# The first two tiles of a feed-forward stage prepared between the heads of the convolution before it

## The chip, the cores and the metric

One NeuronCore of a Trainium2 chip runs the whole program. The metric is device time in microseconds (us) of one execution; lower is better. The engines are TensorE (PE; its weight loads are listed as PEld), VectorE (DVE), ScalarE (ACT), GpSimd (POOL) and SyncE (SP), which here only issues DMAs. Each engine runs its own instructions strictly in order, and they meet through semaphores.

## What is computed

One decoder layer on x of shape (8, 256, 512), in three residual steps. The third and the second matter here.

```python
x = x + attn(layernorm(x), Wq, Wk, Wv, Wo)
x = x + xattn(ctx, ctx, layernorm(x), ssm_kernel, D)      # 32 heads of 8 channels, causal convolutions of length 512
x = x + ffn(layernorm(x), w_gate, w_up, w_down, subln_weight)

def ffn(x):
    gate = bit_linear(x, w_gate); up = bit_linear(x, w_up)   # activations to 8-bit steps by row maximum,
    a = up * square(relu(gate))                              # weights to -1, 0, 1
    a = a * rsqrt(mean(square(a)) + 1e-6) * subln_weight
    return bit_linear(a, w_down)
```

## The kernel before

The program has an attention stage and then one block in which the convolution stage (`convolve`, head by head) and the feed-forward stage (`ffn`, tile by tile) follow each other on every engine.

**Convolution.** There are 32 heads, in pairs: an even head uses buffer 0 of everything and PSUM banks 0 to 3, an odd head buffer 1 and banks 4 to 7. For one head SP loads a Toeplitz matrix (`load_toeplitz`, L754) and the context channels (L759); POOL and ACT form the 36 products of channel pairs (L772, L777 and L920); PE convolves them with 10 matmuls, listed as 20 passes (`convolutions`, L784); ACT empties the upper part of the banks into `ys` (L915, L916) and lays out the queries in `qd` (L927); POOL multiplies a shifted share into `z` (L876); DVE multiplies the rest straight from the banks (`multiply`, L826 and L829) and sums 8 products for each output (`add_up`, L837), into `qo`. `multiply` of head h is the last reader of the banks of head h, so PE may start head h+2 only after it (semaphore `s_z1`, L906). DVE's order is multiply of head h, then add_up of head h-1. ACT also turns the feed-forward's weights into -1, 0, 1, three pieces of 48 in each pair of heads (`ternary`, L935 and L939). ACT's row of a pair is: empty even, squares, piece, queries for the next even head, piece, empty odd, squares, piece, queries for the next odd head. The queries wait for `s_z1` and for POOL's share of the head before (L925, L926). All of it is in hardware loops over pairs (L857, L890, L904, L954, L966); only the last pair stands outside on SP, DVE and ACT.

**Feed-forward.** Its rows are 16 tiles (turns) of 128 rows. The rows of a tile are prepared by a chain: PE transposes the tile's piece of `qo` (L1138); DVE adds it to the residual (`rows_x2`, L1243), takes mean and variance (L1248, L1253, L1257); POOL raises to -1/2 (L1407); DVE normalises (L1263), takes the greatest of each row (L1267) and small factors of it (L1271 to L1280); the row is scaled, rounded to whole numbers and written as bf16 in `xq`; a DMA transpose brings it into `xqt` (`turn_rows`, L1086), which PE needs. The first two tiles need only heads 0 to 15. Before, their chains stand behind the last heads: tile 0 altogether (DVE L1376 to L1395, with the integers on DVE, a transpose on PE, L1144, and a copy on ACT, L1206), tile 1 partly there and partly in turn 0.

A turn has four chunks of 512 columns. For each PE makes gate and up (8 matmuls, L1169), ACT makes relu and its square (L1191, L1193), DVE multiplies the two (`chunk`, L1296), ACT sums squares (L1202), POOL multiplies with the gain (`weigh`, L1411), DVE takes the greatest (`greatest`, L1300). At the end of a tile DVE forms its scale (L1306 to L1326), ACT quantises (L1215), POOL makes bf16 (`integers`, L1419), a DMA transposes it (L1078), and PE multiplies it with the third weight, 16 matmuls at the end of the turn two later (`down`, L1154); DVE adds the result (L1334). In turn t the engines also prepare rows of tiles t+1 and t+2. Turns 0 to 5 and the last two are written out, turns 6 to 13 are a loop (L1049 to L1059).

The buffers of the convolution serve again: `toep` holds the chunks, `kv` the relu results, `big` the weighed tile, the fourth quarter of the weight staging tile `wst` is idle in the convolution, and the gain is loaded over all four quarters in one DMA (L1091) after the last weight piece.

## Time and profile before

| what | value |
|---|---|
| median of 3 runs | 653.18 us (651.61 to 656.78) |
| the profiled execution | 651.45 us, of which the instructions' span is 649.7 us |
| PE busy | 584.2 us, 90% of the span |
| DVE, ACT, POOL busy | 484.3, 457.4 and 363.0 us |
| mean granted PE clock | 0.968 of full speed |

Times in the rows further down are microseconds from the start of the span. A row of a timeline gives start, duration, engine, source line, operation, output and inputs, how many instructions were merged, and in brackets the idle time of the engine before it and what ended that.

### The profile page before, as it was taken

The numbers are of one execution on the slowest core, as the hardware profiler recorded it, in microseconds if no ns is written. First come the engines' busy times: TensorE is split into PE (matmuls) and PEld (weight loads), VectorE is DVE, ScalarE is ACT, GpSimd is POOL, SyncE is SP. The second block draws the span as 40 slices with busy tenths as digits, with TensorE's granted clock in tenths as the row PEclk, the third lists the DMA queues.
The fourth block names the chain that finished last, engine by engine and source line by source line (L and its number), as shares of the span: only waits on it lengthen the run. The fifth ranks groups of instructions, "written<-read, shape, count | busy, mean of one in ns | idle before, by whom it ended". The sixth has DMA issues, their size and how long they took to land.

```text
span 649.7 us, 10218 instructions
## 1 busy us (share of the span) xinstructions
PE 584.2 (90%) x2590; PEld 325.8 (50%) x2590; DVE 484.3 (75%) x936; ACT 457.4 (70%) x783; POOL 363.0 (56%) x327
## 2 busy tenths in 40 slices
PE   5699999999999987979999999965799999999975
PEld 3354453635454542467777777742344434444432
DVE  2737778778878765447877877888889989989860
ACT  1164677676666774178898898864788888888960
POOL 1043626254453625457777777743577777777761
PEclk9889999999999995999999999997899999999997
DMA  8774255546474642055665665532153543533424
GB/s 295 229 226 116 67 118 175 129 161 167 152 212 118 190 106 80 25 159 156 183 181 165 178 185 160 168 88 76 31 106 97 98 99 97 121 97 83 98 66 101
DMA packets 87976, 87.08 MB, mean 134 GB/s; under 512 B 46288, under 2 KB 62160, under 8 KB 87824
## 3 DMA queue, kind: packets, MB, share of 16 engines
q1 hardware_dynamic: 87952, 86.81, 49.2%
q8 instruction: 9, 0.15, 0.1%
q14 instruction: 15, 0.12, 0.1%
HBM read 51.71 MB, written 4.28 MB: 86 GB/s over the span
## 4 chain that ended last, share of the span: by engine, by line
PE 28%; POOL 8%; DVE 8%; issue 6%; DMA 4%; ACT 1%; DVEq 0%; POOLq 0%; SPq 0%; ACTq 0%
PE ps L784 20%; PE ps L1154 5%; POOL big L1411 3%; PE ps L1169 3%; DMA act8t<-ys 3%; POOL ys L1419 2%; DVE toep L1296 2%; DVE st L1248 1%; DVE qo L837 1%; DVE ot L1334 1%; POOL r L1407 1%; DVE x_all L1243 1%; DMA toep<-krows 1%; POOL xq L1426 1%; ACT kv L1193 0%
## 5 line engine op out<-in xcount | busy, mean ns | idle before, releaser
L784 PE MATMUL ps<-kv,toep 128*128 128x288 f32 x640 | 155.8, 406 | 2.0 <-PEq L1482 1.1
L784 PEld LDWEIGHTS ps<-kv,toep 128*128 128x128 f32 x640 | 121.4, 190 | 36.5 <-issue 3.2
L1169 PE MATMUL ps<-wt,xqt 128*128 128x512 bf16 x512 | 120.5, 386 | 13.1 <-DVE toep L1296 6.7
L716 POOL TENSOR_TENSOR pts<-big 128x512 f32<-128x512 f32 x64 | 84.9, 1336 | 58.5 <-ACT big L434 58.2
L434 ACT ACTIVATE big<-ps,kscale 128x512 f32<-128x512 f32 x128 | 85.7, 687 | 43.2 <-PE ps L273 41.2
L1411 POOL TENSOR_TENSOR big<-toep,wst 128x512 f32<-128x512 f32 x64 | 82.7, 1294 | 51.5 <-DVE toep L1296 50.9
L1169 PEld LDWEIGHTS ps<-wt,xqt 128*128 128x128 bf16 x512 | 49.4, 99 | 75.9 <-DVE toep L1296 13.0
L273 PE MATMUL ps<-qx,kx 128*128 128x512 f32 x128 | 76.9, 626 | 9.7 <-DMA qx<-kv 7.9
L837 DVE TENSOR_REDUCE qo<-big 128x2048 f32 (+1 forms) x32 | 72.3, 2259 | 0.0
L593 DVE RECIPROCAL yt<-ps 128x256 f32<-128x256 f32 (+1 forms) x24 | 54.8, 2285 | 20.4 <-PE ps L293 20.4
L1154 PE MATMUL ps<-wt,act8t 128*128 128x512 bf16 x256 | 59.8, 388 | 10.9 <-DMA act8t<-ys 10.0
L772 POOL TENSOR_TENSOR kv<-ctx 128x768 f32<-128x768 f32 (+1 forms) x32 | 52.6, 1644 | 30.0 <-PE ps L784 27.3
L826 DVE TENSOR_TENSOR big<-ps,qd 128x1024 f32<-128x1024 f32 x32 | 39.2, 1224 | 36.5 <-ACT ys L916 34.0
L876 POOL TENSOR_TENSOR big<-ys,qd 128x768 f32<-128x768 f32 x32 | 56.4, 1762 | 14.0 <-ACT ys L916 11.8
L242 PE MATMUL ps<-wq_s,qo 128*128 128x512 f32 x128 | 64.2, 592 | 0.0
L313 PE MATMUL ps<-wo_s,yt 128*128 128x512 f32 x128 | 57.9, 594 | 0.0
L1191 ACT ACTIVATE kv<-ps 128x512 f32<-128x512 f32 x64 | 37.7, 589 | 23.2 <-PE ps L1169 23.1
L273 PEld LDWEIGHTS ps<-qx,kx 128*128 128x128 f32 x128 | 25.0, 199 | 55.7 <-issue 30.9
L1296 DVE TENSOR_TENSOR toep<-ps,kv 128x512 f32<-128x512 f32 x64 | 43.7, 682 | 8.0 <-ACT kv L1193 6.7
L699 POOL TENSOR_TENSOR ro<-ve,half 128x2 f32<-128x2 f32 x8 | 5.5, 692 | 76.8 <-DVE ve L604 76.8
L1154 PEld LDWEIGHTS ps<-wt,act8t 128*128 128x128 bf16 x256 | 24.5, 99 | 44.6 <-DMA act8t<-ys 12.7
L1300 DVE TENSOR_REDUCE mb<-big 128x1 f32<-128x512 f32 x64 | 43.4, 678 | 1.1 <-POOL big L1411 1.0
(127 smaller groups left out, 964.0 us busy)
## 6 DMA issues: line engine op xcount, KB each, us to landing
qx<-kv SPq DMA_DIRECT2D x128, 128.0 KB, 2.4
wst<-in_wall SPq DMA_DIRECT2D x12, 1024.0 KB, 7.1
wst<-in_wall SPq DMA_DIRECT2D x48, 256.0 KB, 3.6
toep<-krows SPq DMA_DIRECT2D x32, 256.0 KB, 3.6
ctx<-in_ctxt SPq DMA_DIRECT2D x32, 192.0 KB, 2.5
qo<-in_xt SPq DMA_DIRECT2D x8, 512.0 KB, 3.9
out_y<-ot SPq DMA_DIRECT2D x16, 256.0 KB, 2.2
conv_part<-qo SPq DMA_DIRECT2D x14, 256.0 KB, 2.8
```

The costliest lines, as they stand in the source:

```text
L242: mm = pe.matmul(MB[:, t, :], rows[:, k, t * P:(t + 1) * P], wq_s[:, k, :], start=(k == 0), stop=(k == CK - 1))
L273: pe.matmul(SB[:, n % 2, :], kx[:, kv, s * P:(s + 1) * P].bitcast(F32R), qx[:, kv, gp * C:(gp + 1) * C].bitcast(F32R), start=True, stop=Tr ...
L313: mm = pe.matmul(OB[:, t, :], yt[:, k, t * P:(t + 1) * P], wo_s[:, k, :], start=(k == 0), stop=(k == CK - 1))
L434: act.activation(pt[:, s, kv, gp * C:(gp + 1) * C], SB[:, n % 2, :], ACT.Exp, scale=kscale[:, c:c + 1]).then_inc(s_e.sem, 1)
L716: nc.gpsimd.tensor_tensor(pts[:, n % 6, :], pt[:, 0, kv, gp * C:(gp + 1) * C], pt[:, 1, kv, gp * C:(gp + 1) * C], ALU.add).then_inc(s_ps.s ...
L784: mm = pe.matmul(m.ps[:, LB * r + lb, :].rearrange("p (b s) -> p b s", s=WIDE)[:, :, 0:PAIRS], m.toep[r][:, d * P:(d + 1) * P], m.kv[r][:, ...
L837: nc.vector.tensor_reduce(qo[:, :, bass.ds(h * HD, HD)], z[r][:], AX.X, ALU.add).then_inc(s_red.sem, 1)
L876: nc.gpsimd.tensor_tensor(z[r][:, :, :, HD - SHIFTS:HD].rearrange("p n j s -> p n s j"), window(ys[r][:], SHIFTS - 1, (SHIFTS * EW, NB), ( ...
L1154: mm = pe.matmul(DB, act8t[r][:, k, :], down_w[:, k, :], start=(k == 0), stop=(k == FK - 1))
L1169: mm = pe.matmul(bank[:, n % 2, :], xqt[r][:, k, :], wt[:, k, n * C:(n + 1) * C], start=(k == 0), stop=(k == CK - 1))
L1296: nc.vector.tensor_tensor(a[n % 2][:], UB[:, n % 2, :], r2[n % 2][:], ALU.mult).then_inc(s_a.sem, 1)
L1411: nc.gpsimd.tensor_tensor(act_w[r][:, n * C:(n + 1) * C], a[n % 2][:], gb[:, n * C:(n + 1) * C], ALU.mult).then_inc(s_w.sem, 1)
```

## The change

The convolution's hardware loops end after head 17 on PE, DVE, POOL and SP (`EARLY = 9` pairs); heads 18 to 31 are written out in the feed-forward's part of each engine. ACT keeps its loop. Into the written-out heads go the two row chains, a step per head:

- PE transposes tile 0's piece of `qo` ahead of head 20 and tile 1's ahead of head 25, each into bank 1 of that head's own four banks; that head then computes its blocks in the order 3, 2, 0 and, after DVE's addition, 1.
- DVE does one step of a chain ahead of the multiply of each head: addition (heads 19 and 24), statistics (20, 25), normalising and greatest (21, 26), factors (22, 27), integers (23, 28). The normalised row goes to SBUF instead of a bank.
- POOL's power stands behind its share of heads 20 and 25.
- SP's DMA transposes of the two rows stand behind the whole SP turn of heads 24 and 25, and between the Toeplitz loads of heads 30 and 31. The PE transpose of tile 0, its copy on ACT and the bf16 identity go.
- PE's turn 0 starts behind head 31 when head 30's banks are free. The transposes for tile 2 follow chunk 1 of turn 0 and wait for the multiply of head 31.
- DVE no longer sums heads 30 and 31 ahead of turn 0: `add_up` of head 30 stands in turn 1 behind chunk 1, that of head 31 in turn 2 behind chunk 3. Two of tile 0's four `greatest` move from turn 0 to turn 1.
- ACT's last weight piece moves into turn 0, between `square` of chunk 0 and the relu of chunk 2; two pieces stand ahead of emptying head 31.
- The gain is loaded in four DMAs, the first early, into the idle quarter, the others behind the last three weight pieces, all ahead of the `conv_part` load for tile 3.
- ACT's and POOL's share of tile 2's integers move to the front of turn 1.

```diff
+EARLY = 9
...
-def convolutions(pe, m, r):
-
-    for lb in range(LB):
+def convolutions(pe, m, r, blocks=range(LB)):
+
+    for lb in blocks:
...
-        with pe.Fori(1, PR) as i:
+        with pe.Fori(1, EARLY) as i:
             for r in range(2):
-                pe.wait_ge(s_z1.sem, 2 * i + r - 1)
-                conv(2 * i + r, r, i + 1)
+                conv(i, r)
+        return ready, conv
...
-        for r in range(2):
-            empty(H2 - 2 + r, r)
-        for s in range(3):
-            ternary(PR - 1, s)
+        empty(H2 - 2, 0)
+        ternary(PR - 1, 0)
+        ternary(PR - 1, 1)
+        empty(H2 - 1, 1)
+        return ternary
...
+    HEAD_TURNED = (20, 25)
+    first_banks = [m.ps[:, 1, :], m.ps[:, LB + 1, :]]
...
+        gain(0)
+        for i in range(EARLY, H2 // 2 - 1):
+            conv_turn(i)
+            if i == 12:
+                turn_rows(0, 0, first=True)
+        toeplitz(H2 // 2 - 1, 0)
+        turn_rows(1, 1, first=True)
+        toeplitz(H2 // 2 - 1, 1)
+        for s in range(3):
+            weights(H2 // 2 - 1, s)
         sp.wait_ge(m.s_red.sem, H2 // 2)
         place(2)
-        sp.wait_ge(m.s_tern.sem, PIECES)
-        sp.dma_start(gb[:], g.rearrange("(o n) -> o n", o=1).broadcast_to([P, FF])).then_inc(d_g.sem, 16)
+        for n in range(1, IC):
+            sp.wait_ge(m.s_tern.sem, PIECES - IC + 1 + n)
+            gain(n)
         place_next(3)
-        turn_rows(1, 1, first=True)
...
-                if n == 0 and rows:
+                if n == (0 if after else 1) and rows:
+                    if not after:
+                        pe.wait_ge(m.s_z1.sem, H2)
                     turn_conv_part(t + 2)
...
-        pe.wait_ge(m.s_red.sem, H2 // 2)
+        for h in range(2 * EARLY, H2):
+            if h not in HEAD_TURNED:
+                conv(h // 2, h % 2)
+                continue
+            t = HEAD_TURNED.index(h)
+            pe.wait_ge(m.s_z1.sem, h - 1)
+            pe.wait_ge(m.s_red.sem, H2 // 2)
+            turn_conv_part(t, qo[:, :, t * T:t * T + P], first_banks[t])
+            ready(h, h % 2, h // 2 + 1)
+            convolutions(pe, m, h % 2, (3, 2, 0))
+            wait(pe, s_x2, t, 1)
+            convolutions(pe, m, h % 2, (1,)).then_inc(m.s_conv.sem, 1)
         pe.wait_ge(m.s_z1.sem, H2 - 1)
-        for t in range(2):
-            turn_conv_part(t, qo[:, :, t * T:t * T + P], first_banks[t])
-        pe.wait_ge(c_ident.sem, 2)
-        turn_first_rows()
...
+            if not after:
+                square(t, 0, after)
+                ternary(H2 // 2 - 1, 2)
             relu(t, 2)
...
+        def first_turn():
+            chunk(0, 0, False)
+            chunk(0, 1, False)
+            rows_x2(2)
+            rows_stats(2)
+            rows_mean(2)
+            rows_var(2)
+            greatest(0, 0, 0)
+            chunk(0, 2)
+            rows_norm(2)
+            chunk(0, 3)
+            rows_greatest(2)
+            rows_scale(2)
...
-            chunk(t, 0, after)
+            chunk(t, 0)
+            if not last:
+                greatest(t - 1, 1, 1 - r)
+                greatest(t - 1, 2, 1 - r)
...
+            chunk(t, 1)
+            if not last:
+                add_up(dve, H2 - 2, 0)
+            scale(t - 1, 1 - r)
...
             chunk(t, 3)
+            if last and not final_first:
+                add_up(dve, H2 - 1, 1)
...
+        for h in range(2 * EARLY, H2 - 1):
+            for t in range(2):
+                first_rows(t, h + 1 - HEAD_TURNED[t])
+            dve.wait_ge(m.s_red.sem, h - 1)
+            multiply(dve, h, h % 2)
+            add_up(dve, h - 1, 1 - h % 2)
+        dve.wait_ge(m.s_red.sem, H2 - 2)
+        multiply(dve, H2 - 1, 1)
         schedule(turn, dve.Fori)
...
+        for h in range(2 * EARLY, H2):
+            if h == HEAD_TURNED[0]:
+                pool.wait_ge(c_half.sem, 1)
+            conv_turn(h // 2, h % 2)
+            if h - 2 in HEAD_TURNED:
+                power(rs, ve, s_ve, s_rs, HEAD_TURNED.index(h - 2))
+        for r in range(2):
+            multiply_shifted(H2 - 2 + r, r)
```

How the order of the instructions moves is shown at three places. Names are `line operation output<-inputs shape`; changed lines have new numbers.

DVE in before, from the multiply of head 31 (L826, L829) to the end of tile 0's rows; x_all is the residual, xq0 the finished row:

```order
L826 TENSOR_TENSOR big<-ps,qd1 128x256x4
L829 TENSOR_TENSOR big<-ps,qd1 128x256
L1253 BN_AGGR mv3<-st 128x2
L1257 TENSOR_SCALAR ve<-mv3 128x1
L837 TENSOR_REDUCE qo<-big 128x32x8
L1263 TENSOR_SCALAR ps<-x_all,mv3,rs 128x512
L1267 TENSOR_REDUCE mx<-ps 128x1
...
L1284 TENSOR_SCALAR xq32<-ps,s127 128x512
L1286 TENSOR_SCALAR xq0<-xq32 128x512
```

DVE now, heads 20 to 23 (L827 and L830 are a multiply, L838 an add_up):

```order
L1271 BN_STATS st<-x_all 128x6
L1276 BN_AGGR mv3<-st 128x2
L1280 TENSOR_SCALAR ve<-mv3 128x1
L827 TENSOR_TENSOR big<-ps,qd0 128x256x4
L830 TENSOR_TENSOR big<-ps,qd0 128x256
L838 TENSOR_REDUCE qo<-big 128x32x8
L1288 TENSOR_SCALAR xq32<-x_all,mv3,rs 128x512
L1292 TENSOR_REDUCE mx<-xq32 128x1
...
L1310 TENSOR_SCALAR xq32<-xq32,s127 128x512
L1312 TENSOR_SCALAR xq0<-xq32 128x512
L827 TENSOR_TENSOR big<-ps,qd1 128x256x4
L830 TENSOR_TENSOR big<-ps,qd1 128x256
```

Each step of the chain now stands ahead of a multiply, that is between an add_up and the instruction that frees PE's banks.

DVE in before, turn 1 from chunk 1 of tile 1 (L1296) to its chunk 2; L1306 begins the scale of tile 0:

```order
L1296 TENSOR_TENSOR toep1<-ps,kv1 128x512
L1306 TENSOR_REDUCE sm<-ss 128x1
L1308 TENSOR_SCALAR cc<-cf_all 128x1
L1311 TENSOR_SCALAR var<-sm,cc 128x1
L1313 TENSOR_REDUCE mb<-mb4 128x1
```

DVE now, the same place (chunk is L1351, the scale begins with L1361):

```order
L1355 TENSOR_REDUCE mb4<-big 128x1 x2
L1266 TENSOR_TENSOR x_all<-ps,x_all 128x512
L1355 TENSOR_REDUCE mb4<-big 128x1
L1271 BN_STATS st<-x_all 128x6
L1351 TENSOR_TENSOR toep1<-ps,kv1 128x512
L838 TENSOR_REDUCE qo<-big 128x32x8
L1361 TENSOR_REDUCE sm<-ss 128x1
```

The sum of head 30 (L838) stands between chunk 1 and the scale, and ahead of chunk 1 stand three `greatest` of tile 0 (L1355) where turn 1 of before has one.

SP in before, from the last pair of heads on (L754 Toeplitz, L852 weight pieces, L1064 the piece of qo for PE, L1091 the gain, L1086 a row transpose):

```order
L754 DMA toep0<-krows 128x512
L754 DMA toep1<-krows 128x512
L852 DMA wst2<-in_wall 128x512 x3
L1064 DMA conv_part<-qo 128x4x128
L1091 DMA wst2<-in_g 128x2048
L1064 DMA conv_part<-qo 128x4x128
L1086 DMA_TRANSPOSE xqt1<-xq1 128x4x128
```

SP now, from the end of the SP turn of heads 24 and 25 to the load for head 27, and from the last pair on:

```order
L853 DMA wst2<-in_wall 128x512
L1098 DMA_TRANSPOSE xqt0<-xq0 128x4x128
L755 DMA toep0<-krows 128x512
L760 DMA ctx0<-in_ctxt 128x384
...
L755 DMA toep0<-krows 128x512
L1098 DMA_TRANSPOSE xqt1<-xq1 128x4x128
L755 DMA toep1<-krows 128x512
L853 DMA wst2<-in_wall 128x512 x3
L1076 DMA conv_part<-qo 128x4x128
L1072 DMA wst2<-in_g 128x512 x3
L1076 DMA conv_part<-qo 128x4x128 x2
```

A row transpose now stands in SP's queue ahead of a Toeplitz load of head 26 and another ahead of that of head 31; three gain loads stand ahead of the `conv_part` load for tile 3.

## Rows read from the trace of the kernel before

**Rows 1.** Stage windows: us, busy time of each engine (instructions), PE clock, DMA share, GB/s
```profile
300.00:431.30 131.30, 131.30 (x543) 102.72 (x543) 105.54 (x84) 113.12 (x186) 97.28 (x79) 1.00 0.57 171
431.30:442.70 11.40, 1.56 (x13) 1.08 (x11) 10.96 (x21) 6.06 (x9) 2.73 (x4) 0.68 0.26 92
468.00:479.40 11.40, 10.94 (x52) 5.04 (x53) 10.51 (x31) 10.51 (x20) 9.00 (x9) 1.00 0.39 81
```

**Rows 2.** Chain of waits, heads 2 to 28 of the convolution on PE
```profile
285.67 131.20 PE ps L784 x540
```

**Rows 3.** Timeline of PE, from the last head to turn 4
```profile
431.24 1.04 PE L1138 MATMUL ps<-ident,qo 128*128 128x128 f32 x8
...
442.74 3.26 PE L1169 MATMUL ps<-wt,xqt 128*128 128x512 bf16 x8 [0.77 <-ACT xqt L1206]
...
455.82 3.55 PE L1169 MATMUL ps<-wt,xqt 128*128 128x512 bf16 x8 [2.64 <-DMA xqt<-xq]
...
467.98 1.90 PE L1169 MATMUL ps<-wt,xqt 128*128 128x512 bf16 x8 [2.99 <-DMA xqt<-xq]
...
475.96 3.63 PE L1154 MATMUL ps<-wt,act8t 128*128 128x512 bf16 x16 [0.46 <-DMA act8t<-ys]
479.42 1.89 PE L1169 MATMUL ps<-wt,xqt 128*128 128x512 bf16 x8
...
490.75 1.89 PE L1169 MATMUL ps<-wt,xqt 128*128 128x512 bf16 x8
```

**Rows 4.** Timeline of DVE, heads 27 and 28
```profile
414.51 1.22 DVE L826 TENSOR_TENSOR big<-ps,qd 128x1024 f32<-128x1024 f32 x1 [1.78 <-ACT ys L916]
415.65 0.62 DVE L829 TENSOR_TENSOR big<-ps,qd 128x256 f32<-128x256 f32 x1
416.11 2.26 DVE L837 TENSOR_REDUCE qo<-big 128x2048 f32 x1
418.55 1.23 DVE L826 TENSOR_TENSOR big<-ps,qd 128x1024 f32<-128x1024 f32 x1 [0.19 <-DVE qo L837]
```

**Rows 5.** Timeline of ACT, heads 27 and 28
```profile
413.30 0.89 ACT L915 COPY ys<-ps 128x768 f32<-128x768 f32 x1
...
420.89 0.62 ACT L927 COPY qd<-qo 128x512 f32 x1 [0.56 <-POOL big L876]
```

**Rows 6.** Timeline of DVE, the row chain behind the last head
```profile
432.88 0.69 DVE L1248 BATCH_NORM_STATS2 st<-x_all 128x6 f32<-128x512 f32 x1
...
437.59 0.80 DVE L1263 TENSOR_SCALAR ps<-x_all,mv,rs 128x512 f32<-128x512 f32 x1
...
439.16 0.15 DVE L1271 TENSOR_SCALAR cl<-mx 128x1 f32<-128x1 f32 x1
...
440.04 0.74 DVE L1284 TENSOR_SCALAR xq<-ps,s 128x512 f32<-128x512 f32 x1
...
441.16 0.68 DVE L1243 TENSOR_TENSOR x_all<-ps,x_all 128x512 f32<-128x512 f32 x1
```

**Rows 7.** DMA issues, 400 to 470 us: KB each, median us to landing
```profile
toep<-krows SPq DMA_DIRECT2D x5, 256.0 KB, 3.8
...
xqt<-xq SPq DMA_TRANSPOSE x2, 2.6
```

**Rows 8.** Timeline of SP, the first row transpose
```profile
453.25 1.30 SPq L1086 DMA_TRANSPOSE xqt<-xq  x1
```

**Rows 9.** Timeline of ACT, weight pieces behind the last head, then turn 0
```profile
432.52 0.82 ACT L935 ACTIVATE wst<-wst,magic,wscale 128x512 f32<-128x512 f32 x1
...
434.07 0.80 ACT L935 ACTIVATE wst<-wst,magic,wscale 128x512 f32<-128x512 f32 x1
...
449.53 0.59 ACT L1191 ACTIVATE kv<-ps 128x512 f32<-128x512 f32 x1
...
450.69 0.61 ACT L1202 ACTIVATE asq<-toep 128x512 f32<-128x512 f32 x1
```

**Rows 10.** Timeline of POOL, the first `integers`, in turn 2
```profile
469.57 1.90 POOL L1419 TENSOR_SCALAR ys<-big 128x2048 bf16<-128x2048 f32 x1
```

More of the change, by code:

```diff
@@ L1042, in schedule @@
     def schedule(turn, fori):
-        turn(0, 0, after=False, last=False)
+        turn(0, 0, after=False, last=False, more=False)
         turn(1, 1, last=False)
@@ L1218, in turn @@
             relu(t, 0)
+            if after and not last:
+                rows_scaled(t + 1)
             if after:
@@ L1221, in turn @@
             relu(t, 1)
-            if more:
+            if more and last:
                 rows_scaled(t + 1)
+            if not after:
+                square(t, 0, after)
+                ternary(H2 // 2 - 1, 2)
             relu(t, 2)
-            square(t, 0, after)
+            if after:
+                square(t, 0)
             square(t, 1)
@@ L1428, in turn @@
         def turn(t, r, after=True, last=True, rows=True, more=True, pair=0, stores=0, final_first=True):
+            if not after:
+                for n in range(IC):
+                    pool.wait_ge(d_g[n].sem, 16)
+                    weigh(t, n, r)
+                    if n == 0:
+                        power(rs, ve, s_ve, s_rs, t + 2)
+                return
+            if not last:
+                rows_integers(t + 1, 1 - r, pair + r)
             weigh(t, 0, r)
             weigh(t, 1, r)
[L1431 to L1434 removed]
+            power(r4, var, s_var, s_r4, t - 1)
+            if more and last:
+                rows_integers(t + 1, 1 - r, pair + r)
             if rows:
```

164 lines of the change are left out of this document (65 added, 99 removed).

## Prediction, made before the changed kernel ran

> **What bounds the kernel now.** I first read the busy time by stages. From 300 to 431 us PE is busy for all of its time at the full clock, 2.4 GHz, so the convolution is bound by PE; the 11.4 us behind it hold 1.56 us of PE work at a mean clock of 0.68, while DVE is busy for 10.96 of them; a later turn of 11.4 us has PE busy for 10.94 and DVE and ACT for 10.51 each [rows 1]. So there are three regimes, and the change moves work from the second into the other two. The chain of waits gives the rhythm of the first: 27 heads in 131.20 us without a gap, 4.86 us each, so head 28 ends at 416.87 and the last at 416.87 + 3 x 4.86 = 431.45, near the 431.24 at which PE goes on with the transposes [rows 2, 3]. I call that end E and count from 431.4. The timeline of PE then shows the turns: turn 0 starts at 442.74, that is E + 11.3; turn 1 at E + 24.4, after a wait of 2.64 us for its row transpose; turn 2 at E + 36.6, after 2.99 us for the same reason; turn 3 at E + 48.0, turn 4 at E + 59.35, so the rhythm is then 11.35 [rows 3]. The first 8 matmuls of turns 0 and 1 take 3.26 and 3.55 us, those of turn 2 take 1.90 [rows 3]: PE had been idle and came back at the lower of its two levels, 1.2 GHz.
>
> **What goes.** The gap from E to turn 0 (11.3 us), the two waits for row transposes (2.64 and 2.99 us) and 1.4 and 1.65 us of slow matmuls. They can't be added up as the gain, since work of DVE and ACT comes back elsewhere. I work out the start of turns 1 to 4 anew instead.
>
> **Turn 0 to turn 1: E + 8.3.** PE starts at E: head 30's multiply is long done, and both row transposes were issued heads before. Of ACT's and DVE's work: emptying head 31 takes 1.2 us (from its start to the multiply that waits for it) [rows 4, 5]; a relu and its square 1.16 [rows 9]. Chunk 0's is thus through at E + 2.5, and chunk 1's at about E + 4, since its gate needs 12 matmuls of 0.24 (8 in 1.90 [rows 3]). Then come square (0.8, with its read-out), the moved weight piece, 434.07 - 432.52 = 1.55, and chunk 2's relu pair: E + 7.5 [rows 9]. DVE's chunk (about 0.7) ends near E + 8.3, and PE's turn 1 waits for that. DVE is not later: head 31's multiply ends at E + 3.1 (1.2 + 1.14 + 0.62 [rows 4]).
>
> **Turn 1 to turn 2: 13.0.** Turn 2 waits for chunk 2 of turn 1, one turn of DVE later. A turn is 10.51 us of DVE [rows 1]; added is the sum of head 30, 2.26 [rows 4]; I add 0.25 for the wait for chunk 3's relu. Turn 2 starts at E + 21.3. The row transpose of tile 2, with 2.6 us to land [rows 7], is ready before: its factors are done at E + 11.5, integers and landing follow in about 4.
>
> **Turn 2 to turn 3: 13.0.** Turn 2 now ends with the first `down`. In before `integers` began 469.57 - 467.98 = 1.6 us after the start of turn 2 and `down` 475.96 - 467.98 = 8.0 after it [rows 3, 10]. DVE's scale of tile 0 is the thing that is late now, behind the sum of head 30: POOL comes to `integers` behind the product of chunk 3, at turn 2 + 3.1, so `down` starts at 9.5, and with its 3.45 us (479.42 - 475.96) turn 3 starts at 13.0 [rows 3], E + 34.3.
>
> **Turn 3 to turn 4: 13.0.** The sum of head 31 is one more 2.26 us of DVE ahead of turn 3's first chunk [rows 4]. DVE was some 0.7 us early then, as PE had waited for `down`, so 11.35 + 2.26 - 0.65 = 13.0. Turn 4 starts at E + 47.3, and from there nothing differs from before. Against E + 59.35 that is 12.0 us won. Each start rests on several such steps, so I hold the 12.0 to within 1.5 either way; the two sums that move out of the gap give 4.5 us back, which is the largest cost.
>
> **Heads 18 to 31: E itself gets later.** (a) PE's 8 transposes, 1.04 us [rows 3], now all stand on the path: +1.04. (b) DVE's pieces. A tile costs 0.68 (addition) + 0.69 and two tiny operations, about 1.0 (statistics) + 439.16 - 437.59 = 1.57 + 440.04 - 439.16 = 0.88 + 441.16 - 440.04 = 1.12, 5.25 in all [rows 6], so 10.5 for both. In a pair DVE is idle for 1.78 ahead of an odd multiply and 0.19 ahead of an even one [rows 4]. So the pieces at odd heads (19, 21, 23, 25, 27) are hidden by the wait for ACT's emptying; those at even heads, 1.0 (20), 0.88 (22), 0.68 (24), 1.57 (26), 1.12 (28), push the multiply. What that costs: an odd multiply ends at 415.65 + 0.62 = 416.27, and PE needs it at 416.87, slack 0.6. An even one has 1.4 for PE, but ACT lays out the next even queries behind it, which now wait 0.56 for POOL [rows 5]; a delay beyond that shifts ACT's next piece and the emptying of the odd head. So about 0.56 + 0.6 less 0.15 for the signal, 1.0, is free. Head 26 exceeds it by 0.5; what is not won back in head 27 adds to head 28's 1.12. I take 1.2 for both. Ends: 0, and 10.5 if every piece stood on the path; 1.2 because only two of ten pieces exceed their slack. (c) SP. A Toeplitz load is issued some 0.4 us after the head before last ends and lands in 3.8 [rows 7], so 0.65 of 4.86 is left. The first row transpose holds SP for 1.30 [rows 8] ahead of head 26's load; 0.5 of that is covered by the transposes ahead of head 25. I take 0.1; the ends are 0 and, were the load to wait for the whole landing of the transpose (2.6 + 3.8 + 0.4 - 5.4 [rows 7]), 1.4. The second transpose goes out before head 31's load is due and costs nothing, by the same count. What (a) to (c) do not show is code written out for 14 heads; turns 0 to 5 are written out too, and their rhythm of 11.35 [rows 3] is that of the loop, so 0. Sum: E + 2.3.
>
> The Trainium skill bears on (c). In "DMA: Bandwidth & Descriptors", Queues, rings and completion order, it says that an engine's descriptors are consumed in ring order, a later one behind an earlier. By that the load of head 26 stands behind the transpose, and the sum would be at the upper end of (c); the rows of before show no load behind a transpose on a path, so they neither confirm nor deny it.
>
> Costs taken as nothing: three gain loads ahead of tile 3's `conv_part` (it is then due at about E + 10, just when turn 1's PE comes to it; if late, DVE still has 3 us before it needs the result); POOL's two powers between heads (POOL is busy for 97.28 of 131.3 [rows 1]); two weight pieces ahead of emptying head 31 (3.1 us into ACT's idle time there; without that cover, as if ACT is late by the delay of (b), some tenths).
>
> **Sum.** -12.0 + 2.3 = -9.7. The profiled execution took 651.45 (span 649.7), so 641.75; from the median, 653.18, 1.7 above it, it is 643.5. I say 643. A measurement here tells about 1%, 6.5 us, from no change.
>
> **Rivals.**
> 1. *The prize is halved by the turns* (gain 3 to 6.5, about 648). PE is busy for only half of turns 1 and 2, with waits of up to 3.4 us, and falls to 1.2 GHz as it did before turns 0 and 1; 1.4 to 1.65 us at up to two restarts [rows 3], and (b) at 2 to 3 instead of 1.2. For it: turn 1 of before came back slow behind its wait. Against: turn 2, behind a like wait, ran at the full clock [rows 3], and DVE, not PE, sets these turns. The Trainium skill ("TensorE: Matmul & The Clock Gate", Part 1) says that an idle array goes to half rate and work brings it back, which agrees with the 0.68 in the gap [rows 1]; by it the sum would lose up to 3.
> 2. *DVE becomes the bound of heads 18 to 31* (slower, about 655). Every delayed multiply delays ACT's queries, ACT's emptying and so the next multiply, and the slack is never won back: all 10.5 us of pieces, 1.04 of transposes and 1.4 of the load make 12.9 against 12.0, and a slow restart adds 1.5. It decides once E is over 12 us later. For it: 105.54 of 131.3 us of DVE and 113.12 of ACT are taken [rows 1]. Against: the gap of 1.78 in each pair.
> 3. *More is won* (gain 13 to 15, about 639): the sums hide where DVE waits for `down`, and the pieces cost nothing.
> 4. *It doesn't do what it says*: turn 0 still waits, for a row transpose that comes late. The second is issued two heads before E; no row speaks for it. Then the gain is 3 or less, 651.
>
> **Chances.** Forecast (gain 6.5 to 13) 0.62; rival 1 0.20; rival 2 0.05; rival 3 0.10; rival 4 0.03. Faster by over 1% are the forecast, rival 3 and a little of rival 1: 0.74. Within 1%: 0.23, slower by over 1%: 0.03. The range goes from rival 3 to the upper part of rival 1: 638 to 649.5.
>
> **What would show it.** Right: heads from 18 on at 4.86 us with about 0.5 more at 20 and 25 and a few tenths at 27 to 31; the first gate matmuls directly behind the last head; turns 1, 2, 3, 4 at about 8, 21, 34 and 47 us after it; add_up in turns 1 and 2. Wrong: PE waits of over 1 us at several heads for DVE's multiply (rival 2), 3 us and more for 8 matmuls in turns 1 to 3 (rival 1), a wait for `toep` at head 26 over 1 us, or a turn 1 later than E + 10.

## The result: 644.2 us, and the profile after

The changed kernel takes 644.2 us (median of 4 runs, 642.72 to 645.77) against 653.38 (4 runs, 651.61 to 656.78) for the one before, measured on the same chip: a ratio of 0.9864, with a 95% interval of 0.9829 to 0.9899. The forecast was 643.0, faster; measured is 1.4% faster. The profiled execution took 645.77 us, its span is 643.9 and its mean granted clock 0.976.

Windows of after, one for the heads from 300 us on and one for each of turns 0, 2 and 4 (columns as in [rows 1]: the stretch, its length, the busy time of PE, PEld, DVE, ACT and POOL with the number of instructions, the granted PE clock, the DMA share, GB/s):

```profile
300.00:439.90 139.90, 138.15 (x567) 105.87 (x567) 118.08 (x114) 119.83 (x196) 102.19 (x84) 1.00 0.59 172
439.90:447.90 8.00, 7.31 (x36) 3.46 (x36) 6.82 (x12) 7.58 (x15) 4.59 (x4) 1.00 0.21 73
...
460.60:473.50 12.90, 12.26 (x51) 5.34 (x53) 12.03 (x33) 12.12 (x21) 10.20 (x10) 0.89 0.35 73
...
486.35:497.70 11.35, 10.93 (x52) 5.00 (x52) 10.48 (x31) 10.09 (x19) 8.63 (x8) 1.00 0.45 104
```

The regime in the middle of [rows 1], 11.4 us with 1.56 of PE at a clock of 0.68, is gone: turn 0 has PE busy for 7.31 of 8.00 us at the full clock. In exchange PE is no longer busy all through the heads (138.15 of 139.90), DVE's busy time there is 118.08, and turn 2 has a clock of 0.89.

The timeline of PE in after, heads 2 to 31 and the start of turn 0, which answers to [rows 2] and the top of [rows 3]:

```profile
289.50 77.84 PE L785 MATMUL ps<-kv,toep 128*128 128x288 f32 x320 [0.81 <-DMA toep<-krows]
367.56 9.94 PE L785 MATMUL ps<-kv,toep 128*128 128x288 f32 x40 [0.21 <-issue]
377.33 0.60 PE L1160 MATMUL ps<-ident,qo 128*128 128x128 f32 x4
377.77 15.00 PE L785 MATMUL ps<-kv,toep 128*128 128x288 f32 x60
392.94 9.97 PE L785 MATMUL ps<-kv,toep 128*128 128x288 f32 x40 [0.18 <-DVE big L830]
402.87 0.66 PE L1160 MATMUL ps<-ident,qo 128*128 128x128 f32 x4
403.36 5.02 PE L785 MATMUL ps<-kv,toep 128*128 128x288 f32 x20
408.57 19.92 PE L785 MATMUL ps<-kv,toep 128*128 128x288 f32 x80 [0.20 <-issue]
429.42 5.12 PE L785 MATMUL ps<-kv,toep 128*128 128x288 f32 x20 [0.93 <-DVE big L830]
434.71 5.12 PE L785 MATMUL ps<-kv,toep 128*128 128x288 f32 x20 [0.17 <-DVE big L830]
439.88 2.32 PE L1182 MATMUL ps<-wt,xqt 128*128 128x512 bf16 x10
```

The row that was unbroken in [rows 2] is cut at heads 18 (367.56), 20 and 25 (the transposes), 23 (392.94), 26 (408.57), 30 and 31. Turn 0 (L1182) follows head 31 with no gap. The timeline of PE over turns 1 to 4:

```profile
447.86 1.89 PE L1182 MATMUL ps<-wt,xqt 128*128 128x512 bf16 x8 [0.69 <-DVE toep L1351]
...
455.35 1.90 PE L1182 MATMUL ps<-wt,xqt 128*128 128x512 bf16 x8 [1.30 <-DVE toep L1351]
460.63 3.25 PE L1182 MATMUL ps<-wt,xqt 128*128 128x512 bf16 x8 [3.38 <-DVE toep L1351]
...
470.06 3.63 PE L1170 MATMUL ps<-wt,act8t 128*128 128x512 bf16 x16 [0.54 <-DMA act8t<-ys]
473.52 1.89 PE L1182 MATMUL ps<-wt,xqt 128*128 128x512 bf16 x8
...
486.35 1.89 PE L1182 MATMUL ps<-wt,xqt 128*128 128x512 bf16 x8
```

The waits ahead of turns 1 and 2, for a row transpose in [rows 3], are now for DVE's chunk; turn 2 comes back at the lower level (3.25 us for 8 matmuls instead of 1.90; a granted clock of 0.55 from 460.60 to 463.72), 1.2 GHz, after a wait of 3.38.

For all kernels below (their times are single runs where no interval stands with them) I use three lengths: the time from the start of head 17 to the start of head 31 (by the single weight loads on PE; "a step" is that from one head to the next), the starts of turns 1 to 4 after E (by the first matmul of each turn; E is the end of head 31's last matmul), and, for the net, from the start of head 2 to turn 4. The expectations recorded ahead of the runs count the turns from weight loads, which gives 8.2 and 21.0 for the 8.0 and 20.8 of turns 1 and 2. The net is 204.90 us before and 196.66 after, 8.2 less. Head 2 began between 284.7 and 289.5 us in the thirteen profiles, and last in after's, though the change does not touch what stands ahead of it; so a single time can't tell 1 or 2 us, and the lengths can. The heads of after stand unchanged in three other kernels here (sums_first, no_sums, warm), and the length of heads 17 to 30 in these four profiles is 72.60 to 72.76: it repeats to 0.2 us. Single steps vary more: that into head 18 takes 5.4 to 5.6 there, and that behind head 20 is the shorter (5.2 to 4.9) the longer it is.

| kernel | time, us | heads 17 to 30 | turns 1, 2, 3, 4 after E |
|---|---|---|---|
| before | 653.4 | 67.91 | 24.4, 36.6, 48.0, 59.35 |
| after | 644.2 | 72.60 | 8.0, 20.8, 33.7, 46.5 |
| unroll_only | 653.7 | 68.11 | 24.5, 36.4, 48.1, 60.2 |
| half_early | 645.5 | 71.44 | 8.0, 20.8, 33.7, 46.5 |
| tile1_odd | 643.2 | 70.99 | 8.0, 20.8, 33.7, 46.5 |
| row0_late | 644.5 | 72.14 | 8.0, 20.8, 33.7, 46.5 |
| gain_late | 646.0 | 72.96 | 8.0, 20.8, 34.5, 47.7 |
| strided | 646.1 | 73.40 | 8.0, 20.8, 33.9, 46.5 |
| sums_first | 646.2 | 72.61 | 14.3, 24.9, 37.8, 49.4 |
| no_sums | 639.8 | 72.64 | 8.0, 19.2, 32.5, 43.9 |
| warm | 643.8 | 72.76 | 8.0, 20.8, 34.0, 46.5 |
| all_three | 642.0 | 69.35 | 8.6, 21.3, 34.2, 47.1 |
| all_four | 641.6 | 69.06 | 8.0, 20.8, 33.8, 46.6 |

So 12.8 us are won behind E and 4.7 are lost ahead of it, where the prediction had 12.0 and 2.3. The experiments ask what the 4.7 are, and whether the 12.8 come about as worked out.

### The profile page after: what moved, and what is told of

The parts are those of the page before. It is cut to its first block and busy times, and to the rows that moved or that the text cites. A ratio compares the mean times of both kernels' runs of the same rounds, so it can differ in the third digit from the quotient of the medians.

```text
span 643.9 us, 9966 instructions
## 1 busy us (share of the span) xinstructions
PE 586.8 (91%) x2569; PEld 326.7 (51%) x2586; DVE 485.7 (75%) x938; ACT 456.1 (71%) x781; POOL 362.8 (56%) x324
## 5 line engine op out<-in xcount | busy, mean ns | idle before, releaser
L785 PE MATMUL ps<-kv,toep 128*128 128x288 f32 x640 | 158.0, 407 | 3.6 <-DVE big L830 1.3
L1182 PE MATMUL ps<-wt,xqt 128*128 128x512 bf16 x496 | 118.0, 383 | 13.4 <-DVE toep L1351 11.8
L1456 POOL TENSOR_TENSOR big<-toep,wst 128x512 f32<-128x512 f32 x64 | 82.8, 1296 | 46.6 <-DVE toep L1351 45.8
L1182 PEld LDWEIGHTS ps<-wt,xqt 128*128 128x128 bf16 x512 | 49.0, 98 | 74.9 <-DVE toep L1351 16.0
L838 DVE TENSOR_REDUCE qo<-big 128x256 f32<-128x2048 f32 (+1 forms) x32 | 72.2, 2258 | 0.0
L877 POOL TENSOR_TENSOR big<-ys,qd 128x768 f32<-128x768 f32 x32 | 56.4, 1764 | 17.8 <-ACT ys L921 14.3
L243 PE MATMUL ps<-wq_s,qo 128*128 128x512 f32 x128 | 65.7, 604 | 0.0
L827 DVE TENSOR_TENSOR big<-ps,qd 128x1024 f32<-128x1024 f32 x32 | 39.1, 1223 | 30.5 <-ACT ys L921 27.2
L1351 DVE TENSOR_TENSOR toep<-ps,kv 128x512 f32<-128x512 f32 x64 | 43.6, 682 | 4.8 <-ACT kv L1215 4.6
L1170 PEld LDWEIGHTS ps<-wt,act8t 128*128 128x128 bf16 x256 | 24.4, 99 | 42.6 <-DMA act8t<-ys 13.0
L1224 ACT ACTIVATE asq<-toep 128x512 f32<-128x512 f32 x64 | 39.7, 621 | 6.3 <-DVE sm L1361 4.0
```

The costliest lines, as they stand in the source:

```text
L243: mm = pe.matmul(MB[:, t, :], rows[:, k, t * P:(t + 1) * P], wq_s[:, k, :], start=(k == 0), stop=(k == CK - 1))
L785: mm = pe.matmul(m.ps[:, LB * r + lb, :].rearrange("p (b s) -> p b s", s=WIDE)[:, :, 0:PAIRS], m.toep[r][:, d * P:(d + 1) * P], m.kv[r][:, ...
L838: nc.vector.tensor_reduce(qo[:, :, bass.ds(h * HD, HD)], z[r][:], AX.X, ALU.add).then_inc(s_red.sem, 1)
L877: nc.gpsimd.tensor_tensor(z[r][:, :, :, HD - SHIFTS:HD].rearrange("p n j s -> p n s j"), window(ys[r][:], SHIFTS - 1, (SHIFTS * EW, NB), ( ...
L1170: mm = pe.matmul(DB, act8t[r][:, k, :], down_w[:, k, :], start=(k == 0), stop=(k == FK - 1))
L1182: mm = pe.matmul(bank[:, n % 2, :], xqt[r][:, k, :], wt[:, k, n * C:(n + 1) * C], start=(k == 0), stop=(k == CK - 1))
```

## Experiments on the heads: where the 4.7 us are lost

Three waits of after stood out. The first is around head 19 (timelines of POOL, ACT and DVE in after, one row each):

```profile
373.70 1.63 POOL L773 TENSOR_TENSOR kv<-ctx 128x768 f32<-128x768 f32 x1 [2.17 <-DVE fhalf L1428]
```
```profile
377.55 0.62 ACT L932 COPY qd<-qo 128x512 f32 x1 [1.57 <-POOL big L877]
```
```profile
380.95 1.22 DVE L827 TENSOR_TENSOR big<-ps,qd 128x1024 f32<-128x1024 f32 x1 [2.29 <-ACT ys L921]
```

POOL stands for 2.17 us ahead of its products for head 20, until DVE has set `half`, the exponent -1/2: DVE reaches that line only behind its loop, and POOL's wait for it, which stood ahead of turn 0 before, now stands ahead of these products, two heads ahead of the power that needs the constant. ACT's queries wait for POOL, and the multiply of head 19 for ACT. The second is a cast by DVE of 1.86 us ahead of the multiply of head 28, and the 0.93 and 0.17 us of PE ahead of heads 30 and 31. The third is head 26, whose Toeplitz load goes out behind a row transpose. The wait ahead of head 18 I put down, wrongly, to the end of the loops.

**unroll_only.** The kernel before, with heads 18 to 31 written out on SP, POOL, PE and DVE:

```diff
-        with pe.Fori(1, PR) as i:
+        with pe.Fori(1, 9) as i:
+            turn(i)
+        for i in range(9, PR):
+            turn(i)
```

> The kernel before with heads 18 to 31 written out and nothing else moved. Measure: from the first matmul of head 2 to that of head 31 (before 140.5 us, changed kernel 145.2). Theory (transposes, DVE's pieces, waits and the queue cost the 4.7 us): at most 0.6 over before, the one loop exit. Rival (written-out heads are slow in themselves, 0.13 us each): 1.8 or more over before.

Heads 2 to 31 took 141.09 us against 140.58, so the total is that of the theory; its place is not. The step from head 17 to head 18 takes 4.85 us here (5.41 in after), and the excess lies in three single heads of 5.01, 5.16 and 5.19 us at other places, such as other kernels show inside the loop too (5.0 to 5.25). Heads 17 to 30 take 68.11, 0.2 more than before. The end of the loops costs nothing, as predicted; something else holds head 18 in after.

**half_early.** After, with the constant set ahead of DVE's convolution:

```diff
+        m.set_half()
...
-        nc.vector.memset(half[:], -0.5).then_inc(c_half.sem, 1)
```

> The changed kernel with the constant of POOL's powers set ahead of DVE's convolution instead of behind its loop. Theory (POOL's 2.17 us wait for it ahead of head 20's products makes ACT and then DVE late at head 19): no such wait, and heads 2 to 31 shorter by 0.4 to 1.0. Rival (the slack is won back before the stalls at heads 26 to 30): 0.2 or less.

Heads 2 to 31 take 144.38 us, 0.85 less than in after: the theory holds. Heads 17 to 30 take 71.44, 1.16 less; but 0.29 of that lies at the step into head 18 (5.12 for 5.41), which does not wait for the constant. So its price is 0.85 to 1.16 us. The step behind head 20 falls from 5.12 to 4.72, that behind head 22 from 5.30 to 4.85. With the constant early, tile 0's five pieces on DVE are hidden wholly (the steps behind heads 20 to 23 take 4.72 to 4.85).

**tile1_odd.** After, with tile 1's chain one head later, so that its five pieces fall to other heads of each pair, and its row transpose behind the last Toeplitz load:

```diff
-    HEAD_TURNED = (20, 25)
-    first_banks = [m.ps[:, 1, :], m.ps[:, LB + 1, :]]
+    HEAD_TURNED = (20, 26)
+    first_banks = [m.ps[:, 1, :], m.ps[:, 1, :]]
```

> The changed kernel with tile 1's chain one head later (transposes ahead of head 26, its long steps ahead of odd multiplies) and its row transpose behind head 31's Toeplitz load. Theory (pieces at even heads push the multiply that frees the banks): the gaps behind heads 28 and 29 (0.4 and 1.3) go, heads 2 to 31 shorter by 1.5 to 2.0. Rival (DVE's steps on SBUF wait for POOL wherever they meet, whatever the head): the bf16 cast takes about 1.8 us again and 0.5 or less is won.

Heads 17 to 30 take 70.99 us, 1.61 less. (Heads 2 to 31, the length of the expectation, take 143.88, 1.35 less and so a little under the theory's 1.5; the heads ahead of 17, which the edit does not reach, took 0.2 longer here.) PE, timeline of tile1_odd, from head 26 to turn 0:

```profile
406.06 29.45 PE L785 MATMUL ps<-kv,toep 128*128 128x288 f32 x120 [0.35 <-DMA toep<-krows]
435.56 1.67 PE L1182 MATMUL ps<-wt,xqt 128*128 128x512 bf16 x7
```

The gaps ahead of heads 30 and 31 are gone (120 passes in one row). The cast has no POOL product of 768 columns beside it now and takes 0.55 us; it is the normalising that meets one (1.63 us), at an odd head, where ACT empties until 418.39 and the multiply begins at 418.65. The row transpose that moves too had no price in after: head 31's Toeplitz load, issued behind it at 429.41, landed 1.77 us before the head began. So the 1.6 us are DVE's pieces.

**row0_late.** After, with the transpose of tile 0's row behind the last Toeplitz load. The timeline of SP in after shows what it removes:

```profile
403.43 1.31 SPq L1098 DMA_TRANSPOSE xqt<-xq  x1
404.79 0.57 SPq L755 DMA_DIRECT2D toep<-krows  x1
```

```diff
-            if i == 12:
-                turn_rows(0, 0, first=True)
...
         toeplitz(H2 // 2 - 1, 1)
+        turn_rows(0, 0, first=True)
```

> The kernel after, but the DMA transpose of tile 0's row is issued behind the Toeplitz load of head 31 instead of ahead of the loads of heads 26 and 27. Theory: the load of head 26 is late by the 1.31 us for which the row's transpose holds SP, which costs head 25 to 26 about 0.45 us of PE; heads 2 to 31 take 144.7 to 144.9 us instead of 145.23, and the idle time of PE ahead of head 26 goes. Rival 1: the load stands behind the whole landing of the transpose in the queues; then 1 us or more is won at that place. Rival 2: DVE's late steps at heads 26 to 28 set the end anyway, and nothing is won (145.2).

Heads 17 to 30 take 72.14 us, 0.46 less than after; the step into head 26 falls from 5.29 to 4.72, and the timeline of PE has no break there:

```profile
401.34 24.70 PE L785 MATMUL ps<-kv,toep 128*128 128x288 f32 x100
426.97 5.12 PE L785 MATMUL ps<-kv,toep 128*128 128x288 f32 x20 [0.93 <-DVE big L830]
```

The theory holds. In after the load itself took its ordinary time: it went out at 404.79 and landed 3.69 us later, just before head 26 began at 408.57; in the other seven kernels that keep this order it took 3.7 to 4.0 (3.8 in [rows 7]). What cost was SP's 1.31 us, not a wait for the transpose's landing. The prediction took from the Trainium skill ("DMA: Bandwidth & Descriptors", Queues, rings and completion order) that the sum would be at the upper end of (c), 1.4; the run decides for 0.46. The section speaks of the order in which descriptors are consumed, and adds that a later one may finish its write before an earlier one; a wait for the whole landing does not follow from it.

**gain_late.** After, with the first gain load behind the last weight load. SP in after, ahead of head 18:

```profile
362.85 0.34 SPq L1072 DMA_DIRECT2D wst<-in_g  x1
363.24 0.42 SPq L755 DMA_DIRECT2D toep<-krows  x1
```

```diff
-        gain(0)
         for i in range(EARLY, H2 // 2 - 1):
...
             weights(H2 // 2 - 1, s)
+        gain(0)
```

> The kernel after, but the first of the four gain loads is issued behind the last weight load instead of ahead of the Toeplitz load of head 19's successors (it stands now between the loops and the first written-out turn of SP). Theory: in after this load of 256 KB goes out 0.4 us ahead of a Toeplitz load that has little time left, and makes head 18 late: the step from head 17 to head 18 takes 5.41 us in after and 4.85 in before. Without it that step takes 4.85 to 4.9, and heads 17 to 30 take 72.1 to 72.3 us instead of 72.60. Rival: the late head 18 is the end of the loops (first instructions of written-out code); then the step keeps 5.3 to 5.6 us.

PE, timeline of gain_late, heads 16 to 19:

```profile
354.76 19.32 PE L785 MATMUL ps<-kv,toep 128*128 128x288 f32 x79
373.92 0.60 PE L1160 MATMUL ps<-ident,qo 128*128 128x128 f32 x4
```

The step into head 18 is 4.85 us and the break is gone: the gain load held the Toeplitz load, and the rival falls. (Head 18's load goes out 1.12 us behind the start of head 17 in after and 0.57 here, and lands in 4.23 us there and 2.98 here.) But the total was missed: heads 17 to 30 take 72.96 us, since the step behind head 20, which waits for the constant, takes 5.58 instead of 5.12, and the step into head 26 takes 5.62 (5.29 in after). A gain ahead of another wait is only a longer wait: the steps into head 18 and behind head 20 add up to 10.43 us here and to 10.53 in after.

Turn 4 also started 1.2 us later here. The trace shows PE's granted clock at 0.50 from 458.00, the start of turn 2, to 463.00 (in after it is back at 1.00 from 463.72, 3.1 us into the turn). ACT then waited 2.08 us for PE's matmuls ahead of the relu of chunk 1 (0.52 in after), and DVE 1.10 us for ACT. So the low clock, where it lasts that long, reaches the path. That is read from one profile; all_four, which moves the same load, does not show it.

**strided.** DVE's cast (L1312) and the normalising (L1288), with what POOL does at the same time; timelines of DVE and of POOL in after, and first the cast of before, with POOL idle:

```profile
440.82 0.43 DVE L1286 TENSOR_SCALAR xq<-xq 128x512 bf16<-128x512 f32 x1
```
```profile
400.09 0.56 DVE L1312 TENSOR_SCALAR xq<-xq 128x512 bf16<-128x512 f32 x1
...
414.47 1.17 DVE L1288 TENSOR_SCALAR xq<-x_all,mv,rs 128x512 f32<-128x512 f32 x1
...
425.33 0.48 DVE L1310 TENSOR_SCALAR xq<-xq,s 128x512 f32<-128x512 f32 x1
425.85 1.86 DVE L1312 TENSOR_SCALAR xq<-xq 128x512 bf16<-128x512 f32 x1
427.63 1.21 DVE L827 TENSOR_TENSOR big<-ps,qd 128x1024 f32<-128x1024 f32 x1
```
```profile
399.60 0.76 POOL L778 TENSOR_TENSOR kv<-ctx 128x128 f32<-128x128 f32 x1
...
413.74 1.62 POOL L773 TENSOR_TENSOR kv<-ctx 128x768 f32<-128x768 f32 x1 [0.78 <-PE ps L785]
...
424.92 0.45 POOL L778 TENSOR_TENSOR kv<-ctx 128x128 f32<-128x128 f32 x1
425.58 1.84 POOL L877 TENSOR_TENSOR big<-ys,qd 128x768 f32<-128x768 f32 x1 [0.21 <-DVE qo L838]
```

Add start and duration: the normalising ends at 415.64 and POOL's product at 415.36; the cast at 427.71 and POOL's at 427.42. Both end 0.28 to 0.29 us behind a POOL instruction that was under way when they began. It works the other way too: the scaling ahead of the first cast began at 399.54, before POOL's small product, and that takes 0.76 us instead of 0.45. The cast at 400.09 then ends 0.29 us behind this product, so its 0.56 us hold a short wait as well; alone it takes the 0.43 of before. I supposed that a strided operand would avoid this, and laid the row into every second fp32 element of another buffer (`wide`; the scaling, the normalising and the greatest use it too):

```diff
-            nc.vector.tensor_scalar(xq[t][:], xq32, -MAGIC, None, ALU.add).then_inc(s_xq.sem, 1)
+            nc.vector.tensor_scalar(xq[t][:], wide, -MAGIC, None, ALU.add).then_inc(s_xq.sem, 1)
```

> The kernel after, but the normalised row of the first two tiles is kept in every second fp32 element of its buffer; same sums, same counts of elements. Theory: in after the row's casts and the normalising are long (1.86 instead of 0.56 us, 1.17 instead of 0.62) because DVE, in its fast mode for contiguous SBUF operands, cannot run beside a POOL instruction on SBUF; a strided operand takes the slower mode, in which the two do not exclude each other. Then the cast takes one length, 0.6 to 1.2 us, at both tiles and whatever POOL does, no instruction of a row's step ends with a POOL instruction, and the gap of 1.3 us behind head 29 shrinks by about 1; heads 2 to 31 take 144.1 to 144.9 instead of 145.23 us. Rival: the length comes from contention for SBUF alone, so that the cast beside POOL stays near 1.8 us, about three times that without it, and heads 2 to 31 take 145.2 or more.

DVE, then POOL, timelines of strided at the same place:

```profile
424.56 1.86 DVE L1313 TENSOR_SCALAR xq<-act8t 128x512 bf16<-128x512 f32 x1
```
```profile
424.19 1.95 POOL L877 TENSOR_TENSOR big<-ys,qd 128x768 f32<-128x768 f32 x1
```

The theory's number is missed: the cast takes 1.86 us again, ends again 0.28 behind POOL's product (426.42 and 426.14), and heads 2 to 31 take 146.48. So the stride is not what decides. (The heads are longer than after's mostly at another place: tile 0's row transpose held SP for 2.25 us in this profile, and the step into head 26 takes 6.23 us instead of 5.29.) The rival, plain contention, is not what the rows look like either: it does not explain an end that keeps the same distance to POOL's end. The exclusion stands, and what switches it is not settled by this run.

The Trainium skill ("SBUF — State Buffer", Who interferes with whom) says that VectorE and GpSimd share one pair of ports under an exclusive lock, held for a whole instruction; the rows agree (0.43, 0.56 or 1.86 us, and an end 0.28 us behind POOL's). Its page "VectorE: DVE Perf Modes" (What auto-detection actually checks) makes the mode with both ports depend, for one source and a destination in SBUF, on the counts of the dimensions, and names no unit stride; the strided run agrees with that, and my idea went beyond it.

## Experiments on the turns: how the 12.8 us come about

**sums_first.** After, with both sums ahead of turn 0, where before had them:

```diff
-                add_up(dve, H2 - 2, 0)
...
+        add_up(dve, H2 - 2, 0)
+        add_up(dve, H2 - 1, 1)
         schedule(turn, dve.Fori)
```

> The kernel after, but DVE sums heads 30 and 31 directly behind the multiply of head 31, ahead of turn 0, as it did before. Theory: DVE has no spare time in turns 0 to 3, so the two sums cost about 4.5 us wherever they stand: turn 1 starts some 4.3 to 4.8 us later than in after (E + 12.5 to 13.0, E being the end of head 31), turn 2 some 2.3 later, and turn 4 within 1 us of after (E + 46.5 to 47.5). Rival: the sums lie in waits of DVE in turns 1 and 2 in after, so that ahead of turn 0 they cost their whole 4.5 us and turn 4 starts at E + 50 to 51.

Turn 1 starts at E + 14.3 and turn 4 at E + 49.4, 6.2 and 2.9 us later than in after: turn 1 later than the theory, turn 4 between theory and rival. PE, timeline of sums_first, turn 0:

```profile
445.02 8.12 PE L1182 MATMUL ps<-wt,xqt 128*128 128x512 bf16 x24 [4.14 <-DVE toep L1351]
```

PE waits for the first chunk behind the sums, and its granted clock is then 0.53 from 445.00 to 451.00; at first the place costs more than the sums' 4.5. Of the 6.2, 3.3 are made up by turn 4. The other 2.9 are what moving the sums into the turns is worth, the slow restart included; no run parts the two.

**no_sums.** After, with each of the two sums cut to one of its 32 blocks of outputs (the added argument); the other 31 are left out:

```diff
-                add_up(dve, H2 - 2, 0)
+                add_up(dve, H2 - 2, 0, 1)
...
-                add_up(dve, H2 - 1, 1)
+                add_up(dve, H2 - 1, 1, 1)
```

> The kernel after, but the sums of heads 30 and 31, which stand in turns 1 and 2, add up only one of their 32 blocks of outputs (31 of 32 are left out); all signals stay. Theory, by the steps of the prediction: each sum of 2.26 us stands on DVE's path; turn 2 starts about 2.2 us earlier than in after (E + 18.8 instead of 21.0) and turn 4 3.5 to 4.4 earlier (E + 42.1 to 43.0). Rival 1: half of it is hidden, by waits of DVE in turns 2 and 3 for POOL and for the transfer ahead of the third product; turn 2 then starts 2.2 earlier, but turn 4 only 1 to 3. Rival 2: PE's low clock and its transfers set these turns, and turn 4 moves by less than 1.

Rival 1, nearly: turn 2 starts 1.6 us earlier (2.2 was expected) and turn 4 2.6 (43.9 against 46.5). The two sums, 4.5 us of DVE, cost 2.6 where they stand. POOL's first `integers` in after (two rows) and in no_sums, and PE's first `down` in no_sums (timelines of POOL and PE):

```profile
462.46 1.26 POOL L1456 TENSOR_TENSOR big<-toep,wst 128x512 f32<-128x512 f32 x1 [0.60 <-DVE toep L1351]
463.70 1.89 POOL L1464 TENSOR_SCALAR ys<-big 128x2048 bf16<-128x2048 f32 x1
```
```profile
457.56 1.89 POOL L1464 TENSOR_SCALAR ys<-big 128x2048 bf16<-128x2048 f32 x1
```
```profile
454.45 1.89 PE L1182 MATMUL ps<-wt,xqt 128*128 128x512 bf16 x8 [1.79 <-DVE toep L1351]
...
463.90 3.63 PE L1170 MATMUL ps<-wt,act8t 128*128 128x512 bf16 x16 [0.56 <-DMA act8t<-ys]
```

`integers` begins 3.1 us and `down` 9.45 us after the start of turn 2, as in after (463.70 - 460.63 = 3.07 and 470.06 - 460.63 = 9.43), where the sum of head 30 is in. So that sum is not what makes `down` late in its turn. In after `integers` follows the product of tile 1's last chunk without a wait. Also to be seen: PE's wait ahead of turn 2 is 1.79 us here, and the clock stays at 2.4 GHz (1.89 for 8 matmuls).

**warm.** After, with 16 matmuls added that nobody reads, at the end of turn 1:

```diff
+            if after and not last:
+                for k in range(16):
+                    pe.matmul(m.ps[:, 6, :], xqt[r][:, k % CK, :], wt[:, k % CK, 0:C], start=True, stop=True)
```

> The kernel after, with 16 matmuls more at the end of turn 1 on PE, whose result nobody reads: they fill a part of PE's wait of 3.4 us ahead of turn 2. Theory: DVE, not PE, sets turns 1 to 4, so that PE's low clock at the start of turn 2 has no price: the first 8 matmuls of turn 2 fall from 3.25 to about 1.9 us and turn 4 starts where it did, E + 46.5 within 0.4. Rival: the slow restart is on the path; then turns 3 and 4 start 1 to 1.4 us earlier, E + 45.1 to 45.5.

PE, timeline of warm, the added matmuls and the start of turn 2:

```profile
454.77 3.62 PE L1191 MATMUL ps<-wt,xqt 128*128 128x512 bf16 x16
458.31 1.89 PE L1182 MATMUL ps<-wt,xqt 128*128 128x512 bf16 x8
```

The first 8 matmuls of turn 2 take 1.89 instead of 3.25 us, and turn 4 starts at E + 46.5 as in after. The low clock of after's turn 2 costs nothing (in gain_late, one profile, a longer one reaches the path).

## Versions with the waits taken out together

**all_three.** half_early and tile1_odd together, with both row transposes behind the last Toeplitz load:

```diff
         toeplitz(H2 // 2 - 1, 1)
+        turn_rows(0, 0, first=True)
+        turn_rows(1, 1, first=True)
         for s in range(3):
             weights(H2 // 2 - 1, s)
```

> Both edits, and tile 0's row transpose behind head 31's Toeplitz load too. Theory: the waits add up, heads 2 to 31 take 141.7 to 142.7 instead of 145.2, and the time falls by 2.5 to 3.5 us against the changed kernel, to about 641. Rival (turn 0 and its queue pay it back, as the weight pieces load later): 1 us or less.

642.04 us (6 runs, 640.66 to 643.59), a ratio to before of 0.9822, interval 0.9795 to 0.985. That interval overlaps after's, so the times do not part the two; the medians differ by 2.2 us, a little less than the theory's 2.5. The lengths do: from head 2 to turn 4 it is 194.05 us against 196.66. Heads 2 to 31 take 142.09, as expected. Heads 17 to 30 take 69.35 us, 3.25 less than after, as much as half_early, tile1_odd and row0_late apart (1.16 + 1.61 + 0.46 = 3.23). PE, timeline of all_three, the heads from 2 on:

```profile
287.33 87.94 PE L785 MATMUL ps<-kv,toep 128*128 128x288 f32 x360 [0.30 <-DMA toep<-krows]
375.11 0.60 PE L1164 MATMUL ps<-ident,qo 128*128 128x128 f32 x4
375.55 29.36 PE L785 MATMUL ps<-kv,toep 128*128 128x288 f32 x120
404.75 0.60 PE L1164 MATMUL ps<-ident,qo 128*128 128x128 f32 x4
405.19 29.33 PE L785 MATMUL ps<-kv,toep 128*128 128x288 f32 x120
```

Between the transposes there is no row that waits for DVE. Turn 1 starts 0.5 us later than in after: ACT waited 0.45 and 0.41 us for weight pieces whose loads went out behind the two transposes.

**all_four.** all_three, with the gain load as in gain_late and two weight loads ahead of the transposes:

```diff
+        for s in range(2):
+            weights(H2 // 2 - 1, s)
         turn_rows(0, 0, first=True)
         turn_rows(1, 1, first=True)
-        for s in range(3):
-            weights(H2 // 2 - 1, s)
+        weights(H2 // 2 - 1, 2)
+        gain(0)
```

> The kernel of all_three, with the first gain load behind the last weight load, and two of the last three weight loads ahead of the two row transposes instead of all three behind them. Theory: the step from head 17 to head 18 takes 4.85 instead of 5.27 us, so that heads 17 to 30 take about 68.95 us (69.35 in all_three; 67.91 in before and 1.04 for the transposes); and ACT does not wait for the last weight pieces (0.45 and 0.41 us in all_three), so that turns 1 and 4 start at E + 8.2 and E + 46.5 instead of 8.76 and 47.05. Together 0.8 to 1.0 us less, 641.1. Rival: a transfer is late at another place; nothing is won against all_three (642.0).

641.64 us (6 runs, 639.37 to 645.06), ratio 0.9825, interval 0.9788 to 0.9862: not to be told from all_three by the time. The lengths are those of the theory, 69.06 us of heads and turns 1 and 4 where after has them, to 0.1. Now 1.15 us are left of the 4.7. By the steps, 0.44 and 0.50 of these lie around PE's two transposes and 0.22 at the step into head 31.

## Why the prediction was right, point by point

**What goes, and turns 1 to 4.** The starts were forecast at E + 8.3, 21.3, 34.3 and 47.3, and came at 8.0, 20.8, 33.7 and 46.5: 12.8 us won instead of 12.0. Turn 1 rests on ACT's and DVE's work as worked out (head 31's multiply ends at E + 3.1, as said, though the terms given for it add up to 2.96). The turns of 13.0 came as 12.8, 12.9 and 12.8, but two of their reasons fell. The two sums give back 2.6 us, not 4.5 (no_sums). And `down` comes 9.4 us into turn 2, as forecast (9.5), but not because tile 0's scale stands behind the sum of head 30: without the sum it is 9.45. What remains is the other half of that step: POOL comes to `integers` behind the products of the last two chunks of tile 1, which lie at the start of turn 2 (460.56 and 462.46; turn 2 starts at 460.63) now that this turn does not wait for its row. The agreement is in part luck: without the sums the working gives 47.3 - 4.5 = 42.8 for turn 4, and no_sums came at 43.9. The sums were costed 1.9 us too dear and the rest of the turns 1.1 too cheap.

**E.** It was to be 2.3 us later; heads 17 to 30 are 4.7 longer. This is the error of the prediction, and 12.8 against 12.0 covered a third of it.
- (a) PE's transposes, 1.04: right; all_four has 0.94 left at their steps.
- (b) DVE's pieces, 1.2: the mechanism was right (tile 0's are free, tile 1's at heads 26 and 28 push the multiply, and head 27 does not win it back); the size was taken from the row chain of [rows 6], where the normalised row lies in a bank and POOL is nearly idle. Head 28's piece was costed at 1.12 us and took 0.48 + 1.86 beside POOL's product. tile1_odd, which moves these pieces, wins 1.6. The 0.15 us for a signal has no row of before behind it; in after DVE's multiply ends at 429.37 and PE begins at 429.42.
- (c) SP's row transpose ahead of head 26, 0.1: it cost 0.46. The bounds 0 and 1.4 held.
- Costs taken as nothing: "POOL's two powers between heads" cost 0.85 to 1.16 us, not for their length but for the wait for a constant that came along with the first; half_early shows it. The first gain load was not costed at all: it stands ahead of head 18's Toeplitz load, and the step into head 18 is 0.56 longer for it (gain_late); once the constant is early, 0.29 of that shows in the heads (all_three against all_four). Written-out code: 0, as forecast.

These add up: 1.16, 1.61 and 0.46 by the single edits, 0.29 for the gain load and the 1.15 left in all_four make 4.67 of the 4.69.

**The total.** Net 8.2 us from head 2 to turn 4 in the profiles, 9.2 in the medians, forecast 9.7 from the profile. That the medians come within 0.5 us of the forecast is luck in part: a loss at the heads of twice the forecast size stands against a larger gain in the turns, and the medians hold about 1 us that the profiles do not show between head 2 and turn 4.

**The rivals.** Rival 1's low clock did come at turn 2 (3.25 us), but warm shows that it has no price in after, since DVE sets these turns; where it lasted longer, in gain_late, turn 4 came 1.2 us later. Its other condition, (b) at 2 to 3 us, came about only with the wait for the constant counted in (1.61 and 0.85 to 1.16). Rival 2's waits for the multiply are seen at heads 23, 29, 30 and 31 (steps of 5.27 to 6.04 us), but slack is won back between them, and 4.7 is far from the 12 at which it decides. Rival 3 was right that the sums hide in part; the heads took that back. Rival 4 fell: turn 0 starts directly behind head 31.
